# Attention outputs kept by feature: row sums moved by copies instead of transposes

## What is computed

```python
att = jax.nn.softmax(jnp.where(causal, q @ k.T * hd ** -0.5, -jnp.inf), axis=-1)
att = att * decay_weight_matrix(T)      # attention_a alone: zero from a lag of 511 on
y = jnp.einsum('bhqk,bhkd->bhqd', att, v)      # per head
y = y.transpose(0, 2, 1, 3).reshape(B, T, 256)
return y @ W_proj                       # attention_b: y @ Wo + bo, then a layernorm
```

## Time and profile before

| what | value |
|---|---|
| median of 3 runs (lowest to highest) | 2736.07 us (2735.41 to 2739.4) |
| profiled execution: its own time; span in the profile | 2736.11 us; 2734.4 us |
| mean granted TensorE clock | 0.959 |
| PE, PEld, DVE, ACT, POOL busy | 90%, 51%, 72%, 55%, 38% |
| att_a: one group, O of chunk 3 to the next; PE busy in it | 124.35 us; 118.06 us; 8 groups |
| att_b: one group; PE busy in it | 115.21 us; 112.64 us; 8 groups |

### The profile page before, as it was taken

How to read it: one execution, slowest core, us unless ns; L and a number is a source line. 1 busy time by engine, 2 the same in 40 slices (tenths; PEclk the granted TensorE clock), 3 DMA queues, 4 the chain that set the end, 5 groups by cost and what they waited for, 6 DMA issues and landing times. The chain is left out here.

```text
span 2734.4 us, 44488 instructions
## 1 busy us (share of the span) xinstructions
PE 2454.8 (90%) x13984; PEld 1404.0 (51%) x13984; DVE 1958.3 (72%) x4863; ACT 1515.6 (55%) x3309; POOL 1052.5 (38%) x1274
## 2 busy tenths in 40 slices
PE   4959999999999999969997599999999999997788
PEld 2535545454544545437774355555555555553676
DVE  5667787777787777716663588888888888870786
ACT  1218576776767685734332056666666666664333
POOL 0037777777777777751221301000101001011653
PEclk8969999999999999989998589999999999998999
DMA  4994142332505050033544751423505234102110
GB/s 134 252 144 63 24 56 36 44 51 32 70 11 75 13 69 6 5 114 77 125 96 98 111 75 16 64 38 44 70 15 72 32 51 62 18 7 99 47 54 31
DMA packets 181847, 171.03 MB, mean 63 GB/s; under 512 B 90352, under 2 KB 131056, under 8 KB 180848
## 3 DMA queue, kind: packets, MB, share of 16 engines
q1 hardware_dynamic: 181616, 168.18, 35.0%
HBM read 105.98 MB, written 61.08 MB: 61 GB/s over the span
## 5 line engine op out<-in xcount | busy, mean ns | idle before, releaser
L704 POOL TENSOR_TENSOR att_a_wd<-att_a_wt,decay 128x256 f32<-128x256 f32 (+3 forms) x896 | 754.6, 873 | 259.8 <-PE att_a_po L907 122.7
L742 ACT ACTIVATE att_b_wt<-att_b_ps 128x512 f32<-128x512 f32 (+3 forms) x1280 | 589.4, 539 | 354.6 <-PE att_b_ps L882 352.6
L782 DVE TENSOR_REDUCE att_a_mpart<-att_a_pm 128x1 f32<-128x512 f32 x768 | 513.5, 687 | 132.2 <-PE att_a_pm L860 129.0
L782 DVE TENSOR_REDUCE att_b_mpart<-att_b_pm 128x1 f32<-128x512 f32 x768 | 503.7, 686 | 109.7 <-PE att_b_pm L860 107.7
L860 PE MATMUL att_a_pm<-att_a_kop,att_a_qop 128*128 128x512 f32 (+3 forms) x1280 | 522.6, 426 | 55.6 <-DMA att_a_qop<-att_a_qop 28.2
L742 ACT ACTIVATE att_a_wt<-att_a_ps 128x512 f32<-128x512 f32 (+3 forms) x896 | 430.8, 506 | 218.1 <-PE att_a_ps L885 131.6
L860 PE MATMUL att_b_pm<-att_b_kop,att_b_qop 128*128 128x512 f32 (+3 forms) x1280 | 503.0, 408 | 36.6 <-DMA att_b_qop<-att_b_qop 29.9
L882 PE MATMUL att_b_ps<-att_b_qop,att_b_kop 128*128 128x512 f32 (+3 forms) x1280 | 453.2, 383 | 6.6 <-ACT att_b_wt L742 3.4
L722 POOL TENSOR_SCALAR_AFFINE_SELECT att_b_wt<-att_b_wt 128x512 f32<-128x512 f32 x128 | 81.6, 637 | 867.1 <-ACT att_b_wt L742 867.1
L860 PEld LDWEIGHTS att_a_pm<-att_a_kop,att_a_qop 128*128 128x128 f32 x1280 | 240.6, 193 | 324.6 <-DVE att_a_mpart L782 130.2
L860 PEld LDWEIGHTS att_b_pm<-att_b_kop,att_b_qop 128*128 128x128 f32 x1280 | 246.3, 194 | 277.1 <-DVE att_b_mpart L782 112.0
(11 more groups left out here) (174 smaller groups left out, 2622.6 us busy)
## 6 DMA issues: line engine op xcount, KB each, us to landing
att_a_kop<-qk SPq DMA_DIRECT2D x128, 128.0 KB, 7.7
att_a_qop<-qk SPq DMA_DIRECT2D x128, 128.0 KB, 8.0
att_b_kop<-qk SPq DMA_DIRECT2D x128, 128.0 KB, 6.2
att_b_qop<-qk SPq DMA_DIRECT2D x128, 128.0 KB, 6.8
qk<-qkv_a_qk_hi SPq DMA_DIRECT2D x32, 256.0 KB, 4.7
qk<-qkv_a_qk_lo SPq DMA_DIRECT2D x32, 256.0 KB, 4.5
qk<-mid_qk_hi SPq DMA_DIRECT2D x32, 256.0 KB, 4.0
qk<-mid_qk_lo SPq DMA_DIRECT2D x32, 256.0 KB, 4.5
```

Of the source, the lines that this page charges most:

```text
L704: pool.tensor_tensor(wd[:, kq % 2, j, a:z], wt[:, kq % buffers, j, a:z], keep["decay"][:, u:u + z - a], ALU.mult).then_inc(w_decayed, 1)
L742: act.activation(wt[:, kq % buffers, j, a:CH], pe_[:, seen % EBANKS, 0:CH - a], ACT.Exp)\
L782: dve.tensor_reduce(mpart[:, c, piece, u:u + 1], pm[:, n % MBANKS, 0:w], AX.X, ALU.max, negate=True).then_inc(m_reduced, 1)
```

## The change

The attentions no longer transpose or divide. ACT's copy `y` has two buffers. For each chunk SP issues eight DMAs, two for each head: the 16 feature rows go to DRAM `y`, which is now laid out by head, feature and token; the sum row of 512 goes to a 128x16 tile `scol`, 32 partitions a head. DVE adds the far sums in the same form (`fcol`), inverts, and SP stores the inverse to a DRAM tensor `inverse` (item "SU", in YN's place of the list). The far sums reach the form by a DVE transpose and eight DMAs (item "FT", twice a group in att_a). The PSUM bank of `px` goes to `ps` in att_a (2 to 3 banks) and to `pm` in att_b (3 to 4). In the dense stages `y` arrives with features on partitions; for each chunk 16 further DMAs read an inverse row and spread it over a head's 16 partitions, and DVE multiplies the two into `yt`. PE's transposes and ACT's copy of Y are gone.

```diff
+PIECE = 16
 # attention_plan
-        cost = PV_TIME if item[0] in ("PO", "PV", "YT") else 0.0
+        cost = PV_TIME if item[0] in ("PO", "PV") else 0.0
-            follow(number + 3, GH - 1, ("YT", c))
+            follow(number + 3, GH - 1, ("SU", c))
-    return [x for item in plan for x in ((item, ("YN", *item[1:])) if item[0] == "YT" else (item,))]
+    return [item for _, _, _, item in sorted(timed)]
 # spaced
-                follow((8, 0.0, ("FE", c)), (11, 0.0, ("FM", c)))
+                follow((8, 0.0, ("FE", c)), (11, 0.0, ("FM", c)), (14, 0.0, ("FT", c)))
 # attention
-        MBANKS, EBANKS = (4, 2) if decayed else (3, 3)
+        MBANKS, EBANKS = 4, 3
-        y = sb("y", [P, CH], F32)
+        y = sb("y", [P, 2, CH], F32)
+        scol, inverse = sb("scol", [P, 2, PIECE], F32), sb("inverse", [P, 2, PIECE], F32)
...
 # attention, SP
-                    if item[0] == "YN":
+                    if item[0] == "FT":
+                        _, d, c = item
+                        n = FARS.index(c)
+                        sp.wait_ge(f_turned, len(FARS) * (g + d) + n + 1)
...
+                        for k in range(P // SQUARE):
+                            row = frow[SQUARE * k:SQUARE * k + UNITS, n, :].rearrange("u (i e) -> u i e", e=PIECE)
+                            for i in range(SQUARE // PIECE):
+                                sp.dma_start(fcol[SQUARE // PIECE * k + i::P // UNITS, n, :], row[:, i, :])                                  .then_inc(f_in[n], 16)
+                    if item[0] == "O":
                         c = item[1]
-                        sp.wait_ge(y_ready, done(g, c))
-                        sp.dma_start(dram["y"][g // NG, c][:, :, GH * HD * (g % NG):GH * HD * (g % NG + 1)],
-                                     yn[:, c % 2, :, :]).then_inc(y_out[c % 2], 16)
+                        sp.wait_ge(o_kept, done(g, c) + 1)
...
+                        for j in range(GH):
+                            h, cols = GH * (g % NG) + j, slice(c * CH, (c + 1) * CH)
+                            sp.dma_start(dram["y"][g // NG, h, :, cols], y[STRIP * j:STRIP * j + HD, c % 2, :])\
+                              .then_inc(y_out[c % 2], 16)
+                            sp.dma_start(scol[STRIP * j:STRIP * (j + 1), c % 2, :],
+                                         y[STRIP * j + HD:STRIP * j + HD + 1, c % 2, :].rearrange("o (i e) -> o i e", e=PIECE))                              .then_inc(s_in[c % 2], 16)
+                    if item[0] == "SU":
+                        c = item[1]
+                        sp.wait_ge(s_ready, done(g, c))
+                        sp.dma_start(dram["inverse"][g // NG, g % NG, c].rearrange("j (i e) -> (j i) e", e=PIECE),
+                                     inverse[:, c % 2, :]).then_inc(s_out[c % 2], 16)
 # attention, DVE
-                    if item[0] == "YN":
+                    if item[0] == "SU":
                         c = item[1]
...
+                        dve.wait_ge(s_in[c % 2], S_DMAS * (2 * g + c // 2 + 1))
+                        dve.wait_ge(s_out[c % 2], 16 * (2 * g + c // 2 + 1))
                         if c in FARS:
...
+                            dve.wait_ge(f_in[n], F_DMAS * (g + 1))
+                            dve.tensor_tensor(scol[:, c % 2, :], scol[:, c % 2, :], fcol[:, n, :], ALU.add).then_inc(s_summed, 1)
+                            dve.wait_ge(s_summed, len(FARS) * g + n + 1)
+                        dve.reciprocal(inverse[:, c % 2, :], scol[:, c % 2, :]).then_inc(s_ready, 1)
 # attention, PE
-                    if item[0] == "YT":
...
-                        for t in range(TB):
-                            mm = pe.transpose(px[:, t * P:(t + 1) * P], y[:, t * P:(t + 1) * P], keep["ident"][:, :])
-                        mm.then_inc(y_turned, 1)
 # dense, SP
             def load_y(G):
...
-                sp.dma_start(y[:, G % 2, :, :], at(dram["y"], 0, G)).then_inc(y_in[G % 2], 16)
+                sp.dma_start(y[:, G % 2, :, :], dram["y"][b].rearrange("(k h) d t -> (h d) k t", k=KT)[:, :, cols])\
+                  .then_inc(y_in[G % 2], 16)
+                for h in range(H):
+                    part = slice(HD * (h % (H // KT)), HD * (h % (H // KT) + 1))
+                    sp.dma_start(inverse[part, G % 2, h // (H // KT), :],
+                                 dram["inverse"][b, h // GH, c, h % GH:h % GH + 1, :].to_broadcast([HD, CH])).then_inc(y_in[G % 2], 16)
 # dense, DVE (PE's and ACT's parts of Y are removed)
+                if item[0] == "Y":
+                    dve.wait_ge(y_in[par], Y_LOADS * (G // 2 + 1))
+                    if G:
+                        dve.wait_ge(projected, G)
+                    dve.tensor_tensor(yt[:, :, :], y[:, par, :, :], inverse[:, par, :, :], ALU.mult).then_inc(yt_ready, 1)
```

More of the change, by code:

```diff
@@ L579, in attention @@
         f_done, f_diff, f_factor, f_prod, f_total = (sm(n) for n in ("f_done", "f_diff", "f_factor", "f_prod", "f_total"))
-        y_turned, y_summed, y_inverse, y_ready = sm("y_turned"), sm("y_summed"), sm("y_inverse"), sm("y_ready")
+        f_padded, f_turned = sm("f_padded"), sm("f_turned")
+        f_in = [sm(f"f_in{i}") for i in range(NC - 2)] if decayed else []
+        s_in, s_out = ([sm(f"{n}{i}") for i in range(2)] for n in ("s_in", "s_out"))
+        s_summed, s_ready = sm("s_summed"), sm("s_ready")
         w_masked, w_turn = sm("w_masked"), sm("w_turn")
@@ L759, in step @@
                         act.wait_ge(pv_done, KBS * g + sum(len(near(a, decayed)) for a in range(c + 1)) + buffers)
[L760 to L762 removed]
+                        act.wait_ge(y_out[c % 2], Y_DMAS * (2 * g + c // 2 + 1))
+                        if 2 * g + c // 2:
+                            act.wait_ge(s_in[c % 2], S_DMAS * (2 * g + c // 2))
+                        act.activation(y[:, c % 2, :], po[:, :], ACT.Copy).then_inc(o_kept, 1)
             steps(act, step)
@@ L808, in step @@
                         dve.wait_ge(f_prod, index + 1)
-                        dve.tensor_reduce(ftotal[:, c, :, :].rearrange("p j t -> p (j t)"), ffactor[:, c, 0:n, :].rearrange("p n u -> p u n"),
+                        dve.tensor_reduce(ftotal[:, FARS.index(c), 0:UNITS], ffactor[:, c, 0:n, :].rearrange("p n u -> p u n"),
                                           AX.X, ALU.add).then_inc(f_total, 1)
+                    if item[0] == "FT":
+                        _, d, c = item
+                        n = FARS.index(c)
+                        dve.wait_ge(f_total, len(FARS) * (g + d) + n + 1)
+                        if g + d > 0:
+                            dve.wait_ge(f_in[n], F_DMAS * (g + d))
+                        dve.transpose(frow[:, n, :], ftotal[:, n, :]).then_inc(f_turned, 1)
                     if item[0] == "MC":
@@ L815, in step @@
                         dve.transpose(mrow[:, c, :].bitcast(F32), mneg[:, c, :].bitcast(F32)).then_inc(mrow_ready, 1)
-                    if item[0] == "YN":
+                    if item[0] == "SU":
                         c = item[1]
-                        strips = px[:, :].rearrange("p (t j e) -> p t j e", t=TB, j=GH)
-                        near_sums = strips[:, :, :, HD].rearrange("p t j -> p j t")
-                        dve.wait_ge(y_turned, done(g, c))
+                        dve.wait_ge(s_in[c % 2], S_DMAS * (2 * g + c // 2 + 1))
+                        dve.wait_ge(s_out[c % 2], 16 * (2 * g + c // 2 + 1))
                         if c in FARS:
[L822 to L832, removed]
+                            n = FARS.index(c)
+                            dve.wait_ge(f_in[n], F_DMAS * (g + 1))
+                            dve.tensor_tensor(scol[:, c % 2, :], scol[:, c % 2, :], fcol[:, n, :], ALU.add).then_inc(s_summed, 1)
+                            dve.wait_ge(s_summed, len(FARS) * g + n + 1)
+                        dve.reciprocal(inverse[:, c % 2, :], scol[:, c % 2, :]).then_inc(s_ready, 1)
             steps(dve, step)
@@ L1020, in dense @@
         ROTATION = [item for item in PLAN if item[0] in "HQ"]
-        TURNS = [item for item in PLAN if item[0] in "YXZ"]
+        TURNS = [item for item in PLAN if item[0] in "XZ"]
         PAIRS_USED = [item for item in PLAN if item[0] in "PVB"]
@@ L1299, in _ @@
                 par = G % 2
-                if item[0] == "Y":
-                    act.wait_ge(y_turned, G + 1)
-                    if G:
-                        act.wait_ge(projected, G)
-                    act.activation(yt[:, :, :], pt[:, :, :], ACT.Copy).then_inc(yt_ready, 1)
                 if item[0] == "X":
@@ L1459, in build @@
             "v": dram("v", (B, NG, NC, P, TB * GH * (HD + 1)), F32),
-            "y": chunks(dram("y", (B, T, D), F32)),
+            "y": dram("y", (B, H, HD, T), F32),
+            "inverse": dram("inverse", (B, NG, NC, GH, CH), F32),
             "w1s": dram("w1s", (P, KT, FF), F32), "w2s": dram("w2s", (P, HT, D), F32),
```

44 lines of the change are left out of this document (23 added, 21 removed).

## The result

The changed kernel takes 2883.47 us (median of 4 runs, 2878.01 to 2883.92) against 2737.74 us for the kernel before in the same runs: a ratio of 1.0526, 95% interval 1.0508 to 1.0545. That is 146 us slower. The forecast was 69 us slower, 2805, with a range that ends at 2878: the sign was right, the size was half of what came.

What follows compares the result with a forecast made beforehand. PE was taken to bound attention and mid, a cycle of DVE and PE to bound end. On 2736.1 us, -25-12+67.5+12+19+7.5-5+5 = +69 gave 2805 us, range 2752 to 2878.

Steps and rivals of the forecast that it cites:

- The arrival: Attentions: after eight SP copies the sums land 5.6 us after y ends, 4.9 to 6.5.
- C: Middle of groups: DVE waits 1.6 us for sums; 0.5 x 24 chunks in att_b, nothing in att_a: +12, 0 to 60.
- R1: Rival: waits inside groups are not covered, PE stops for each in both attentions, 72 us for 12: 2865; chance 0.15.
- B: Ends of groups: DVE holds all reductions until the sums land, 4.2 us at 14 ends, plus stage ends: +67.5, 56 to 82.
- The tails: Two ends of attention stages: the inverse must land before the barrier, 4.2 x 2 = 8.5 us.
- A: Middle of groups: PE's removed transposes give back 0.53 us, 48 times: -25, bounds -25 to -10.
- Banks: Attentions: one more PSUM bank for pm in att_b and ps in att_a: -12, bounds -40 to 0.
- R2: Rival: the fourth pm bank halves weight loads' waits, 93 us in att_b, 25 for ps: 2699; chance 0.06.
- R3: Rival: the eight copies issue quickly, sums land 1.75 us after y: 2714; chance 0.04.
- D: Starts of dense stages: more DMAs ahead on SP delay mid by +19 (14 to 25), end by +7.5 (5 to 9).
- E in mid: Mid's steady state: PE loses eight transposes a chunk, 1.06 us, over six chunks: -5, bounds -6 to 0.
- E in end: End's steady state: Y's 1.2 us go onto DVE, in the cycle, 1 us x 5 chunks: +5, bounds 0 to 6.

Runs made afterwards that it cites:

- late_turns: su_late with the PSUM banks of before and four unread transposes of y back on PE at each SU of chunks 0 to 2: 2769.24 us.
- su_end: The change with only chunk 3's SU moved, some two blocks into the next group's list: 2791.49 us, ratio 1.0201.
- su_late: su_end with the SUs of chunks 0 to 2 also two blocks later: 2734.03 us, ratio 0.9980.
- warm: The change with unread matmuls filling PE's idle time at groups' starts and in end, waits left as they are: 2874.37 us.
- turns: banks with four unread transposes of y put back on PE at SU's place, chunks 0 to 2 of each group: 2912.88 us.
- banks: The change with the PSUM banks of before for pm and ps, one bank left idle: 2910.79 us.
- merged: The change with a chunk's four scol copies made one, issued ahead of the four y copies: 2769.81 us, ratio 1.0114.
- ywait: The change with end's multiplication Y on DVE placed just ahead of the addition that waits for P: 2871.01 us.

## Why the prediction was wrong

The runs take the loss apart in one chain of medians: the change 2883, without the waits at groups' ends 2791, without those inside groups 2734, with the banks of before 2752, with the transposes back 2769. (The medians of the kernel before, measured beside them, go from 2737.7 to 2741.8, so each step is good to some 4 us.) The last is still 27 us over before: the dense stages are 37 us longer (12 in mid, 25 in end) and the tails of the attentions 8, so some 18 are given back elsewhere. 14 of them show in late_turns from chunk 3's `y` to chunk 0's (12.50 and 21.43 us in place of 13.67 and 22.27), where chunk 3's transposes and YN's work on DVE stood; which of the two gives them no run shows.

**The arrival was right.** Sums at 5.6 us after `y`, forecast 5.6: in the change they landed at 5.5 to 6.1 at the ends of groups, and at up to 7.6 in the middle, where the loads of 128 KB held them up. The prediction named that as a doubt and gave it no price.

**C was the step that failed.** It let 0.5 us of each wait in att_b through, 12 us in all, and charged att_a nothing. su_end against su_late has 57 us. The waits were longer, 2.5 us in the mean of chunks 0 to 2 of att_b in place of 1.6, and there 45 us of 53 reached the time: the S items and four banks were little cover. That a PE that is 98% busy has no time in which to catch up is the likely reason, argued and not tried alone. That was rival R1, for which the earlier trace rows spoke; R1's time of 2865 was the nearest of all, but partly by luck: it has 72 us for these waits, where 57 were paid, and B and the dense stages as small as in the forecast. "DVE is busy for 94 of 115 us, so it can catch up", which was held against R1, looked at the wrong engine: the time that was lost is PE's.

**B had the right mechanism and too small a size.** 59 us at the ends of groups became 5.9 us a place in att_b and 4.8 in att_a against before, so 75 at seven places each. The fifth M of att_b was later by 3.7 us in the mean of its seven places, as forecast (4.1 at the one shown). What the sum lacked is the clock's fall behind the stop, 1.6 and 0.8 us by warm; with the 4.2 taken for a place that comes to 5.8 and 5.0. The tails were 4.0 and 3.7 us longer, 8 for the forecast 8.5.

**A gave nothing in this kernel.** 25 us were to come back; turns against banks, both with the banks of before, has 2. Where DVE's wait holds PE anyway, PE's saved 0.53 us go into the wait; late_turns shows 17 of them once the waits are gone. A and C were added as if they were independent, and they are not.

**Banks** were worth 27 us in the change and 15 to 18 without waits, forecast 12, inside its bounds. Rival R2 wanted 118; it fell. R3 fell with the issues: eight held SP for 4.4 to 5.8 us at each chunk. On this the Trainium skill, "DMA: Bandwidth & Descriptors", section "Issuing engines are not separate DMA queues", calls issue time usually small beside the DMA; here 0.5 to 0.6 stand beside a landing of 1.7, and merged, with one issue ahead of the inversion, took 114 us off. At the start of mid the number of issues was not what counted: 4 in place of 16 gained nothing there.

**D was right.** Mid's first H came 20.8 us later (forecast 19), end's 6.4 (7.5). E in mid gave more than forecast, 1.4 us a chunk, so mid is 12 us longer in sum (forecast 14).

**E in end was mis-sized.** Chunks grew by 3.1 us, not by 1: 1.4 are Y on DVE, which stands in the cycle as the earlier trace rows showed, and 1.7 are P at the lower clock, after PE has idled 1.4 and 1.3 us for the split and the addition that stand behind Y on DVE. (P was so long in four chunks of five; in turns, with the same code of end, in two.) The stage lost 18 us beyond its start in place of 5; warm gave the 1.7 back, ywait brought the chunks to 24.2.

Each term taken at its place in the chain, the forecast of 69 lacks 45 in C (57 for 12), 15 in B (75 and 8 for 67.5), 10 in the dense stages (37 for 26.5) and 8 in A (17 for 25), and has 6 too much for the banks (18 for 12): 69 + 45 + 15 + 10 + 8 - 6 = 141 of the 146; the rest is within what the steps are good to.

What is still open: why att_a pays a third of DVE's waits inside groups where att_b pays them all. Its PE has more idle time (table of before), which fits, but no run tried that alone.

## What to carry to other kernels

Where two engines feed each other through a few buffers and one of them is busy nearly all the time, don't count on catching up when you price a wait of the other. Here 45 us of 53 were paid with PE 98% busy, and 11 of 33 with PE 95% busy. What is saved elsewhere on the busy engine can vanish into that wait too. A chain through DMAs should not stand in the order where its start was, but where its end is; moved by two blocks, the same instructions waited for nothing. Count the issues in a row ahead of the DMA that is waited for: one that carries all, issued first, was worth 114 us here, and the transposes saved on PE 2 to 17.

## What the runs showed of the hardware

- After 5.5 us without work TensorE's granted clock was 0.50, the lower of its two levels, for about 5 us, and the M matmul took 0.79 us in place of 0.40. In end, behind idle times of 1.4 and 1.3 us, the granted clock was 0.68 in the mean of P, which took 5.38 us, and 1.00 in ywait, where P took 3.69.
- A copy of 2 KB landed 1.7 us after its issue in the median of 128, and 4.3 us after it in the median of four that were issued behind loads of 128 KB.
- Four DMAs that spread 128 KB each held SP for 8.5 us behind 2 MB of loads, and sixteen of 32 KB in the same place for 8.3. With only the load of y ahead, four took 2.5 us and sixteen 7.4.
- A copy from 4 partitions of 512 to 128 partitions of 16 was seen by DVE 1.94 us after its issue began, one of 1 partition to 32 1.65 us after.
